# A new order of the causal score chunks, and FFN evictions alternated between VectorE and ScalarE

## The reference

```python
# x: (8, 2048, 1024)
queries, keys, values = x @ Wq + bq, x @ Wk + bk, x @ Wv + bv      # 1024 wide, one head
logits = einsum('bik,bjk->bij', queries, keys)                    # causal: j <= i
probs  = softmax(logits, axis=1) / sqrt(1024)                      # over i, the QUERY axis
x = layernorm(x + (x + einsum('bij,bjv->biv', probs, values)))
s = x @ Win + bin_                                                # 1024 -> 64
h = relu(s[..., None] * W1 + b1)                                  # 64 x 16 = 1024 hidden
g = einsum('btmh,mh->btm', h, W2) + b2                            # 1024 -> 64
x = layernorm(x + (g @ Wout + bout))                              # 64 -> 1024
```

## Time and profile before

| what | value |
|---|---|
| median of 2 runs | 421.39 us (421.16 to 421.62) |
| the profiled execution | 420.79 us, of which the span of its slowest core (core 7) 419.2 us |
| spans of the 8 cores | 414.7 to 419.2 us |
| busy, core 7 | TensorE 341.9 us (82%), VectorE 185.7 (44%), ScalarE 108.7 (26%) |
| HBM | 31.02 MB read, 12.58 MB written |

### The profile page before, as it was taken

The page is one execution under the profiler, slowest core; times in us unless marked ns, Lnnn a source line. Parts: engine busy times, 40 slices in busy tenths (PEclk is TensorE's granted clock), DMA queues, the critical chain, the costliest instruction groups (busy, mean ns, idle before and its releaser), DMA issues.

```text
span 419.2 us, 4405 instructions; the slowest of 8 cores (414.7 to 419.2 us)
## 1 busy us (share of the span) xinstructions
PE 341.9 (82%) x1488; PEld 148.8 (35%) x1488; DVE 185.7 (44%) x353; ACT 108.7 (26%) x159; POOL 15.5 (4%) x27
## 2 busy tenths in 40 slices
PE   0588999999999999999999964999996583867610
PEld 0233444444444444444444441444442120212200
DVE  0025444444444333332655656542322828656481
ACT  0000000000000000002233222754613375487871
POOL 8000000500000000000000000000000000000000
PEclk9999999999999999999999996999999556567655
DMA  7999960692000000019940000007250656013438
GB/s 91 168 163 154 156 102 2 79 145 28 0 2 0 0 2 0 2 36 286 324 156 2 0 2 0 1 27 165 100 112 1 147 153 102 0 51 150 186 120 297
DMA packets 33542, 36.80 MB, mean 88 GB/s; under 512 B 19824, under 2 KB 24048, under 8 KB 33520
## 3 DMA queue, kind: packets, MB, share of 16 engines
q1 hardware_dynamic: 23616, 25.24, 20.8%
q0 software_dynamic: 9904, 11.28, 19.6%
HBM read 31.02 MB, written 12.58 MB: 104 GB/s over the span
## 4 chain that ended last, share of the span: by engine, by line
PE 60%; DVE 12%; ACT 11%; issue 8%; DMA 5%; DVEq 0%; POOL 0%; ACTq 0%; SPq 0%; POOLq 0%
PE ps L301 36%; PE ps L401 12%; DVE negmax_s L422 5%; ACT probsT L375 5%; PE ps L274 4%; DMA wb<-wq 3%; PE ps L574 3%; DMA af<-abf 2%; PE ps L588 2%; PE ps L362 2%; PE ps L550 2%; ACT a_roll L506 2%; ACT HT L697 1%; DVE ps L416 1%; ACT junk_s L492 1%
## 5 line engine op out<-in xcount | busy, mean ns | idle before, releaser
L301 PE MATMUL ps<-xf,wb 128*128 128x512 bf16 x448 | 96.9, 379 | 2.8 <-DVE Qf L315 2.8
L401 PE MATMUL ps<-V_bf,probsT 128*128 128x512 bf16 x272 | 62.0, 391 | 5.7 <-DVE stream L447 5.7
L362 PE MATMUL ps<-Qf,Kf 128*128 128x512 bf16 (+3 forms) x320 | 60.8, 351 | 5.9 <-ACT probsT L375 4.9
L301 PEld LDWEIGHTS ps<-xf,wb 128*128 128x128 bf16 x448 | 43.8, 98 | 55.9 <-issue 3.2
L301 PE MATMUL ps<-wb,xf 128*128 128x512 bf16 x256 | 55.4, 379 | 0.0
L375 ACT ACT_TABLE_LOAD x1 | 1.3, 1283 | 196.1 <-DVE negmax_s L422 196.1
L315 DVE TENSOR_SCALAR Qf<-ps,bqT_s 128x512 bf16<-128x512 f32 x32 | 23.4, 749 | 52.2 <-PE ps L274 29.0
L362 PEld LDWEIGHTS ps<-Qf,Kf 128*128 128x128 bf16 x320 | 30.1, 100 | 36.7 <-issue 8.5
L401 PEld LDWEIGHTS ps<-V_bf,probsT 128*128 128x128 bf16 x272 | 27.1, 100 | 40.2 <-issue 10.5
L319 DVE TENSOR_SCALAR Kf<-ps,bkT_s 128x512 bf16<-128x512 f32 x32 | 24.0, 751 | 31.2 <-PE ps L301 31.2
L323 DVE TENSOR_TENSOR V_bf<-ps,bvb_s 128x512 bf16<-128x512 f32 x32 | 22.1, 692 | 33.1 <-PE ps L301 33.1
(11 more groups left out here) (61 smaller groups left out, 169.4 us busy)
## 6 DMA issues: line engine op xcount, KB each, us to landing
stream<-x SPq DMA_DIRECT2D x1, 8192.0 KB, 30.7
z<-stream SPq DMA_DIRECT2D x16, 512.0 KB, 4.4
xf<-xt POOLq DMA_DIRECT2D x4, 1024.0 KB, 28.7
abf<-a_roll SPq DMA_DIRECT2D x16, 256.0 KB, 2.1
wb<-wq POOLq DMA_DIRECT2D x8, 256.0 KB, 16.1
wb<-wk POOLq DMA_DIRECT2D x1, 2048.0 KB, 50.1
wb<-wv POOLq DMA_DIRECT2D x1, 2048.0 KB, 18.9
bvb_s<-bvb POOLq DMA_DIRECT2D x1, 256.0 KB, 50.5
```

Of the source, the lines that this page charges most:

```text
L301: ins = t.matmul(ps[:, bank * 512:(bank + 1) * 512], lhsT, rhs, start=(kc == 0), stop=(kc == NDC - 1))
L362: ins = t.matmul(ps[:, boff + soff: boff + soff + sw], Kf[:, kc * T + jc * 128: kc * T + jc * 128 + 128], Qf[:, kc * T + jc * 128 + soff: ...
L401: ins = t.matmul(ps[:, boff + vt * 512: boff + vt * 512 + 512], probsT[:, COFF[jc] + (it - jc) * 128: COFF[jc] + (it - jc) * 128 + 128], V ...
```

## The change

First, the order of the score chunks becomes 12, 13, 14, 15, 0, 1, ... 11 on all engines; the widths, the PSUM banks and the work of each chunk stay. `stt` 0 and 1 still stand ahead of the last chunk in the order, which is now chunk 11. Second, the `htev` of every block is shared: VectorE takes HT tiles 0, 2, 4, 6, ScalarE takes 1, 3, 5, 7, and `gT` waits for both.

```diff
-    JCO_POS = {jc: pos for pos, jc in enumerate(range(16))}
+    JCO_POS = {jc: pos for pos, jc in enumerate([12, 13, 14, 15] + list(range(12)))}
-    JCO_SCHED = list(range(16))
+    JCO_SCHED = [12, 13, 14, 15] + list(range(12))
 # fv_seq, VectorE's FFN list
-        lambda b: [("stev", b)] + ([("htev", (m, b)) for m in range(NDC)]
-                                   if b < 2 else []),
+        lambda b: [("stev", b)] + [("htev", (m, b))
+                                   for m in range(0, NDC, 2)],
 # fa_seq, ScalarE's FFN list
-        lambda b: [("htev", (m, b)) for m in range(NDC)] if b >= 2 else [],
+        lambda b: [("htev", (m, b)) for m in range(1, NDC, 2)],
-        JCO = list(range(16))
+        JCO = [12, 13, 14, 15] + list(range(12))
 # TensorE, HT and gT
-                    bank_set((bank,), "VA"[0 if b < 2 else 1],
-                             fv[("htev", (m, b))] if b < 2
+                    bank_set((bank,), "VA"[m % 2],
+                             fv[("htev", (m, b))] if m % 2 == 0
                              else fa[("htev", (m, b))])
-                    if b < 2:
-                        t.wait_ge(sV, fv[("htev", (7, b))])
-                    else:
-                        t.wait_ge(sA, fa[("htev", (7, b))])
+                    t.wait_ge(sV, fv[("htev", (6, b))])
+                    t.wait_ge(sA, fa[("htev", (7, b))])
```

## The result

| | before | after |
|---|---|---|
| median, us | 421.14 (18 runs) | 422.06 (19 runs) |
| ratio, 95% interval | | 1.0026 (1.0017 to 1.0036) |
| span of the slowest core, us | 419.2 (core 7) | 420.4 (core 1) |

I had forecast 1.2 us less. By the ratio it is 1.1 us more (0.26% of 421.14; the medians themselves lie 0.9 apart): small, but on the other side, and the interval excludes zero. In some executions half of the cores run at a lower granted clock and take some per cent longer, as in one of the 19 here (474.01 us); ratios leave such executions out, and so do the medians of before given with the experiments. Times in the rows of the kernel after are those of its slowest core, core 1, whose projections end 0.35 us earlier than core 7's did.

A forecast was written before the change was run, and what follows sets the result against it. TensorE carries 60% of the chain, but the VectorE and ScalarE loop bounds the scores and TensorE isn't block 0's bound; -5.3 + 9.5 - 3.5 - 1.9 = -1.2, giving 420.2 us on the median's footing, range 416.8 to 424.4.

The forecast's parts named there:

- Term 1: Scores: narrow chunks first start the VectorE and ScalarE loop earlier, so the reads end earlier: -5.3 us.
- Term 2: FFN block 0: ScalarE's odd evictions wait behind work held by the third transposed load, stopping TensorE at HT 5: +9.5 us.
- Rival 1: Block 0: the stall isn't paid, leaving the other gains: -10.7 us, 410.7 us; chance 0.03.
- Term 3: FFN block 1: shared evictions gain 2.5 us and full clock from gtev to stev another 1.0: -3.5 us.
- Term 4: FFN blocks 2 and 3: gtev comes earlier, VectorE becomes the bound, 0.95 us kept in each: -1.9 us.
- Rival 2: TensorE in blocks 1 to 3: the lower clock stays and HT binds: +3.3 us, 424.7 us; chance 0.20.
- variant with only block 1 slow: HT runs at clock 0.50 in block 1 alone of blocks 1 to 3: sum +0.6 us.

The follow-up runs named there:

- the last pair: Two kernels with new chunk order, block 0 evicted by VectorE, timed against the kernel before: blocks 1 to 3 shared, 412.84 us; only block 1 shared, 414.28 us.
- the direct pair: Same-chip comparison, new order, block 0 on VectorE: blocks 1 to 3 shared (ratio 0.9806) beside only block 1 shared (0.9840), ratios to the kernel before.
- The fillers: 18 matmuls adding nothing to the output, put in TensorE's gaps in blocks 1 to 3: kernel after 418.38 us (0.9932), kernel before 421.30 us (0.9972).

## Why the prediction was wrong, point by point

- **Term 1, -5.3 (score order): right.** -5.16 in the trace, the median of the cores; alone, 6.0 by the timing. The slack of TensorE was as thin as worked out, and the loop grew by 0.17 us.
- **Term 2, +9.5 (block 0): right.** +9.3 over the cores, and 9.3 us come back when VectorE keeps that block. Rival 1 is out.
- **Term 3, -3.5 (block 1): the step that failed first.** It measured -1.6 by the medians (on core 7 alone 19.25 to 16.74, -2.5). Its first part, 2.5 us from the evictions, held: `gtev` came 2.3 us earlier, and HT of block 1 began at full clock on seven cores of eight, as I had expected, though on core 1 it fell to 0.50 in its second half. What failed is the second part, "the part from `gtev` to `stev` also falls from 8.22 to block 2's 7.25". It was 8.11 us after the change. And there was little to gain: the 19.25 and the 8.22 from which I subtracted were those of cores 6 and 7; six cores had `out` of this block at full clock already, and the medians were 18.23 and 7.25. In the same way "all at 0.50, and then the clock stood at 1.00 at 370" is true of cores 6 and 7, not of the kernel. Why `out` of block 1 is fast on one core and slow on another isn't shown: it differs as much between two kernels that do the same work there (five and three cores in the last pair).
- **Term 4, -1.9 (blocks 2 and 3): mis-sized.** It measured -0.7 (-0.1 and -0.55), in the direct pair of runs about -1.0. The earlier `gtev`, twice 0.95, was right: 0.9 and 1.0 measured, and VectorE is the bound, 8.42 against 8.46 on core 1. What failed is the tacit term of zero for what follows `gtev`. The earlier trace rows had it at 7.25 with `out` at full clock; shared, it takes 8.0 to 8.1 with `out` at 0.50. The gain of an eviction was paid back a few microseconds later by a slower engine that nobody had touched, and the direct pair shows that this comes with the sharing.
- **Rival 2** named that mechanism, and its +3.3 was too much: HT began at full clock in 19 of the 24 blocks 1 to 3 of the eight cores. The truth, +1.1, lies between my forecast and this rival. Its variant with only block 1 slow, +0.6, came closest in number, but by luck: that was not what happened, as blocks 2 and 3 were slow behind `gtev` too. I gave the full clock as the likelier on the ground of one sequence in one core's trace.
- The fillers show cause, not only company: they raise the clock and take 4.0 us from the kernel after, 1.2 from the one before. Why the clock changes where it does stays open.

The balance of the change: 5.2 us of idle removed, 9.3 us of wait put in, 2.3 us gained behind it: +1.8 over the median core, +1.1 as timed. Leave the first block out of the sharing and the change is worth -8.3 us, as timed.

## What to carry to other kernels

Before sharing work between two engines, look at what stands ahead of it in the second engine's list at that moment: an engine that is 26% busy can be the one that waits 10 us for a DMA, and with rotating buffers its partners wait with it. Where a chain depends on TensorE's clock, read a stage on all cores, and put a range of a microsecond on each pass of such a ring rather than one core's value. A stage that got faster can slow the next one: check the stage behind it for its granted clock before the gain is booked. A loop of dependent engines that can't start before its first item is ready should start with its smallest one, if the engine that feeds it then still keeps ahead, as it just did here: that was worth 1.4% alone.

## What the runs showed of the hardware that I had not expected

- More work made the kernel faster: 18 matmuls without a use, in gaps of about 1 us, gave 0.94% after the change and 0.28% before it (in the kernel after, `out` began at granted clock 1.00 in 19 of 24 blocks instead of 5).
- Sharing the evictions between two engines, with TensorE's own work unchanged, put `out` of blocks 2 and 3 at the lower level: full clock in 2 of 16 cases instead of 15, in two pairs of kernels, for 0.8 to 0.9 us in block 2.
- The same instructions behind the same waits take 16.0 to 17.6 us for one FFN block on different cores of one run, by where the granted clock changes level.
- In one group of runs cores 4 to 7 reached the end of the reads 1.5 to 2 us later than cores 0 to 3, with the same instructions.
